# A perceiver layer on one core: products of zeros, another order of the opening, and row sums on GpSimd

## The reference

```python
x = x + xattn(layernorm(x), ctx, top_k=32)      # ctx: 16 x 512 x 512
# xattn: q = n @ Wq.T + bq; k = ctx @ Wk.T + bk; v = ctx @ Wv.T + bv
#   scores = q @ k.T / sqrt(512); all but the 32 largest of a row are dropped
#   softmax, times v, @ Wo.T + bo
x = x + wave(layernorm(x))   # q, k, v, gate; a decaying-cosine kernel per head
#   exp(-softplus(damping) t) * cos(frequency t + phase), heads mixed by softmax(coupling)
x = x + ffn(layernorm(x))    # weights rounded to -1, 0, 1 by their mean magnitude
```

## Time and profile before

| | |
|---|---|
| Median of 3 runs | 445.98 us (445.91 to 446.12) |
| The profiled execution, its own time | 447.19 us |
| Its span in the profile | 445.4 us |
| Busy: TensorE products, weight loads | 433.1 us, 312.7 us |
| Busy: VectorE, ScalarE, GpSimd | 257.6 us, 205.6 us, 111.1 us |
| First product | 4.33 us |
| First context chunk | 50.41 us |

### The profile page before, as it was taken

One profiled execution on the slowest core, in us unless ns is written; L12 is line 12 of the kernel. 1 busy time (PEld: TensorE's weight loads), 2 busy tenths in 40 slices (PEclk: granted clock), 3 DMA queues, 4 the chain that ended last, 5 costly groups with the idle time before them and its releaser, 6 DMA issues.

```text
span 445.4 us, 5681 instructions
## 1 busy us (share of the span) xinstructions
PE 433.1 (97%) x2045; PEld 312.7 (70%) x2045; DVE 257.6 (58%) x519; ACT 205.6 (46%) x305; POOL 111.1 (25%) x163
## 2 busy tenths in 40 slices
PE   5999999999999999899999999999999999999996
PEld 2587644557565655478888888887888888888884
DVE  2988535567766777769987335548753333533334
ACT  1796852645464466538875445435531111111110
POOL 2600440000000002010008603334256633333330
PEclk9999999999999999999999999999999999999999
DMA  6999920675414542225649000000000000200002
GB/s 192 409 379 391 371 80 0 208 266 190 179 46 155 190 156 105 94 96 188 213 166 177 13 22 4 0 0 1 0 1 0 0 1 1 95 1 1 1 0 94
DMA packets 26844, 49.97 MB, mean 112 GB/s; under 512 B 6208, under 2 KB 6208, under 8 KB 25792
## 3 DMA queue, kind: packets, MB, share of 16 engines
q1 hardware_dynamic: 26816, 49.61, 31.7%
HBM read 47.49 MB, written 2.11 MB: 111 GB/s over the span
## 4 chain that ended last, share of the span: by engine, by line
PE 78%; DMA 7%; DVE 6%; ACT 4%; issue 2%; SPq 1%; POOL 1%; DVEq 0%; ACTq 0%
PE bank L1189 10%; PE bank L1191 10%; PE bank L1190 10%; PE bank L1605 7%; PE bank L1603 7%; PE bank L1589 6%; PE bank L1590 6%; PE bank L1384 6%; PE bank L1370 5%; PE bank L1398 5%; PE bank L1297 3%; PE bank L1196 3%; DMA wab<-w1T 2%; DMA wab<-w2T 2%; DVE ln_s L779 1%
## 5 line engine op out<-in xcount | busy, mean ns | idle before, releaser
L754 ACT ACTIVATE g<-bank,b1c 128x512 f32<-128x512 f32 x32 | 22.0, 688 | 92.0 <-PE bank L1605 92.0
L1169 DVE CAST g_hi<-g 128x512 fp32r<-128x512 f32 x32 | 14.0, 436 | 74.7 <-ACT g L754 74.6
L417 POOL TENSOR_TENSOR ln_rs<-ln_ve,neg_half 128x1 f32<-128x1 f32 x24 | 14.9, 620 | 146.2 <-DVE ln_ve L783 145.8
L1603 PE MATMUL bank<-xt_lo,w1s 128*128 128x512 f32 x128 | 50.8, 397 | 0.0
L1605 PE MATMUL bank<-xt_hi,w1s 128*128 128x512 f32 x128 | 50.7, 396 | 0.0
L1589 PE MATMUL bank<-w2s,g_lo 128*128 128x512 f32 x128 | 50.3, 393 | 0.2 <-DVE g_lo L1171 0.2
L1590 PE MATMUL bank<-w2s,g_hi 128*128 128x512 f32 x128 | 50.0, 390 | 0.0
L569 ACT ACTIVATE mt<-bank 128x512 f32<-128x512 f32 x56 | 30.1, 600 | 28.6 <-PE bank L1370 28.6
L464 POOL TENSOR_SCALAR w2s<-w2t 128x512 fp32r<-128x512 int8 x32 | 19.9, 622 | 65.8 <-PE bank L1590 65.8
L1384 PE MATMUL bank<-mt,qT 128*64 128x512 f32 x128 | 31.1, 605 | 0.0
L1589 PEld LDWEIGHTS bank<-w2s,g_lo 128*128 128x128 f32 x128 | 24.0, 188 | 6.1 <-issue 0.6
(11 more groups left out here) (231 smaller groups left out, 1015.3 us busy)
## 6 DMA issues: line engine op xcount, KB each, us to landing
ctxr<-ctx SPq DMA_DIRECT2D x8, 1024.0 KB, 10.9
ctx<-ctx SPq DMA_DIRECT2D x8, 1024.0 KB, 7.7
wab<-w1T SPq DMA_DIRECT2D x4, 1024.0 KB, 11.5
wab<-w2T SPq DMA_DIRECT2D x4, 1024.0 KB, 9.0
wgraw<-wgT SPq DMA_DIRECT2D x4, 1024.0 KB, 6.5
wst<-w1T SPq DMA_DIRECT2D x4, 1024.0 KB, 4.7
wst<-w2T SPq DMA_DIRECT2D x4, 1024.0 KB, 5.2
resid<-x SPq DMA_DIRECT2D x4, 512.0 KB, 6.9
```

The lines of the kernel that those rows point to most:

```text
L1603: pe.matmul(bank[n % 2][:, :], w1s[:, n % 2, d, :], xt_lo[:, d, half(n // FC)], start=(d == 0), stop=False)
```

## The change

- TensorE multiplies a tile of zeros eight times before the first weight step. GpSimd clears that tile (mix_hi, not yet used) first of all.
- The loads: weights of step 1 go ahead of the first x tiles, and each x load goes one step later. The four small wave inputs are issued by ScalarE's queue, after the first weights have landed. Wv goes ahead of magnitude piece 5 instead of 6. The wait for the lag tables goes behind context 7.
- TensorE turns tiles 0 and 1 before step 3, and tiles 2 and 3 between its two halves. Tiles 4 and 5 and the bias products go behind query products 0 and 1, tiles 6 and 7 behind product 2; x_bias goes one product later, norms behind the first four chunks.
- VectorE takes low parts of tiles 0 to 3 and of M before the statistics of tiles 4 to 7; the low parts of tiles 6 and 7 go behind sum_q and the damping chain. [...] norm_part and token sums 4 and 5 go into the first pair.
- GpSimd makes the cosine's arguments after the deviations of all tiles.
- ScalarE's parts follow the same order. Two magnitude passes go ahead of tiles 4 and 5, and passes 6 and 7 go into the first pair.

The diff, without declarations, the count that consts waits for, and function bodies that only change place:

```diff
@@ SyncE
-            def first_loads(o):
+            def first_weights(o):
                 sp.dma_start(wqraw[:, o, :], rows(wq)[:, o, :]).then_inc(wqk_in[o], 16)
                 sp.dma_start(wkraw[:, o, :], rows(wk)[:, o, :]).then_inc(wqk_in[o], 16)
-                if o == 0:
-                    sp.dma_start(cols[:, :, :], small[0]).then_inc(small_in, 16)
-                    for n, a in enumerate((freq, damp, phase)):
-                        sp.dma_start(wpar[:, n, :], a.partition_broadcast(P)).then_inc(par_in, 16)
-                    sp.dma_start(cpl[0:H, :], coup).then_inc(par_in, 16)
+
+            def x_load(o):
+
                 sp.dma_start(resid[:, 2 * o:2 * o + 2, :], x_v[:, 2 * o:2 * o + 2, :]).then_inc(x_in[o], 16)
...
-            for o in range(DC):
-                first_loads(o)
+            first_weights(0)
+            sp.dma_start(cols[:, :, :], small[0]).then_inc(small_in, 16)
+            for o in range(1, DC):
+                first_weights(o)
+                x_load(o - 1)
+            x_load(DC - 1)
...
-                        if k == 2 * DC - 2:
+                        if k == 2 * DC - 3:
                             sp.dma_start(wvraw[:, :, :], rows(wv)).then_inc(wv_in, 16)
...
-                if b == 4:
+                if b == 7:
                     sp.wait_ge(lag_ok, 2)
                     sp.wait_ge(tpos_ok, 5)
@@ GpSimd
+            pool.memset(f(mix_hi[:, :]), 0.0).then_inc(consts, 1)
             link(pool.memset(ident[:, :], 0.0))
...
+            for t in range(NT):
+                rstd(t)
+
             pool.wait_ge(tpos_ok, 4)
             pool.wait_ge(par_in, 64)
...
-            for t in range(NT):
-                rstd(t)
+            def row_sum(to, raw, col, o):
+
+                scale = cols[:, col, o:o + 1]
+                if o == 0:
+                    return pool.tensor_scalar(to[:, :], raw[:, o, :], scale, None, ALU.mult)
+                link(pool.tensor_scalar(row_part[:, :], raw[:, o, :], scale, None, ALU.mult))
+                return pool.tensor_tensor(to[:, :], to[:, :], row_part[:, :], ALU.add)
+
+            pool.wait_ge(wo_in, 16)
+            pool.wait_ge(qbias_ok, 1)
+            for o in range(DC):
+                row_sum(sum_k, woraw, 2, o).then_inc(sums_ok, 1)
+                pool.wait_ge(sums_ok, DC + o + 1)
@@ ScalarE
+            act.wait_ge(wqk_in[0], 32)
+            for n, a in enumerate((freq, damp, phase)):
+                act.dma_start(wpar[:, n, :], a.partition_broadcast(P)).then_inc(par_in, 16)
+            act.dma_start(cpl[0:H, :], coup).then_inc(par_in, 16)
...
-            first_tiles((0, 1, 2, 3, 4, 5))
-            first_xt((0, 1, 2, 3))
-            first_tiles((6, 7))
-            for e in range(DC):
-                m1_hi_part(e)
...
-            first_xt((4, 5))
-            abs_part(0)
-            first_xt((6, 7))
+            first_tiles((0, 1, 2))
+            first_xt((0,))
+            first_tiles((3,))
+            first_xt((1,))
+            m1_hi_part(0)
+            m1_hi_part(1)
+            first_xt((2, 3))
+            m1_hi_part(2)
+            m1_hi_part(3)
+            abs_part(0)
+            abs_part(1)
+            first_tiles((4, 5))
             act.wait_ge(sp_u, 1)
             act.activation(wtmp[:, 1, :], wtmp[:, 0, :], ACT.Exp, scale=-1.0).then_inc(sp_u, 1)
...
+            first_xt((4, 5))
+            first_tiles((6, 7))
             act.wait_ge(qbias_ok, 1)
             q_part(0)
-            abs_part(1)
             q_part(1)
-            abs_part(2)
             act.wait_ge(sumq_ok, DC)
             q_part(2)
+            first_xt((6, 7))
+            abs_part(2)
+            q_part(3)
             abs_part(3)
-            q_part(3)
...
+            q_part(4)
             abs_part(4)
-            q_part(4)
+            q_part(5)
+            q_part(6)
             abs_part(5)
-            q_part(5)
-            abs_part(6)
-            q_part(6)
             q_part(7)
...
                 if i == 0:
+                    abs_part(6)
                     abs_part(7)
+                    act.wait_ge(abs_ok, 2 * DC)
                     wvo_hi_part(0)
@@ VectorE
-            dve.wait_ge(par_in, 64)
...
-            for o in range(DC):
-                sumk_part(o)
-                first_stats((2 * o, 2 * o + 1))
-            first_xt((0, 1, 2, 3))
-            for e in range(DC):
-                m1_lo_part(e)
+            sumk_part(0)
+            first_stats((0, 1))
+            sumk_part(1)
+            first_stats((2, 3))
+            sumk_part(2)
+            first_xt((0, 1))
+            m1_lo_part(0)
+            m1_lo_part(1)
+            first_xt((2, 3))
+            m1_lo_part(2)
+            m1_lo_part(3)
+            first_stats((4, 5))
+            sumk_part(3)
+            first_stats((6, 7))
+            dve.wait_ge(par_in, 64)
...
+            first_xt((4, 5))
             dve.wait_ge(qbias_ps, 1)
             dve.tensor_copy(qbias[:, :], bank[4][:, 0:DC + 1]).then_inc(qbias_ok, 1)
-            first_xt((4, 5))
             for o in range(DC):
                 row_sum(sum_q, wqraw, 1, o).then_inc(sumq_ok, 1)
                 dve.wait_ge(sumq_ok, o + 1)
-            first_xt((6, 7))
...
             link(dve.scalar_tensor_tensor(out=a, in0=q, scalar=2.0, in1=a, op0=ALU.mult, op1=ALU.add))
+            first_xt((6, 7))
...
-            xbias_sum()
             token_part(6)
             token_part(7)
             mix_part()
             token_part(0)
-            xbias_part()
             token_part(1)
...
             token_part(3)
+            xbias_part()
...
                 if i == 0:
+                    norm_part()
+                    token_part(4)
+                    token_part(5)
...
                     wvo_lo_part(0)
@@ TensorE
-            def m1_step(o):
+            def m1_step(o, es=range(DC)):
...
+            pe.wait_ge(consts, 1)
+            for n in range(8):
+                pe.matmul(bank[7][:, 0:P], f(mix_hi[:, :]), f(mix_hi[:, :]), start=True, stop=True)
             for o in range(DC - 1):
                 m1_step(o)
-            pe.wait_ge(consts, 4)
-            for t in range(4):
-                turn_first(t)
-            m1_step(DC - 1)
+            pe.wait_ge(consts, 5)
+            turn_first(0)
+            turn_first(1)
+            m1_step(DC - 1, (0, 1))
+            turn_first(2)
+            turn_first(3)
+            m1_step(DC - 1, (2, 3))
...
+            pe.wait_ge(xt_lo_ok, 4)
+            q_product(0)
+            q_product(1)
             turn_first(4)
             turn_first(5)
-            pe.wait_ge(xt_lo_ok, 4)
-            q_product(0)
+            query_bias()
+            q_product(2)
             turn_first(6)
             turn_first(7)
-            q_product(1)
-            q_product(2)
+            q_product(3)
...
-            for n in range(3, 2 * DC):
+            for n in range(DC, 2 * DC):
                 if n == 5:
                     coupling()
-                if n == 6:
+                if n == 7:
                     x_bias()
-                if n == 7:
-                    norms()
                 q_product(n)
...
                     ln2_turn(i - 3)
+                if i == 0:
+                    norms()
                 score(i, 0)
```

More of the change, by code:

```diff
@@ L145, in perceiver_kernel @@
          (cvt_hi, cvt_lo, gate, bias_2, w1s, w2s, g32, g_hi, g_lo),
-         (wab, turns, sum_k, sum_q, bias_x)) = region(
+         (wab, turns, sum_k, sum_q, bias_x, row_part)) = region(
             [("wvo_hi", [P, DC, D], F32R), ("wvo_lo", [P, DC, D], F32R),
@@ L531, in abs_part @@
                 act.activation(v, v, ACT.Abs, accum_out=wabs[:, k:k + 1]).then_inc(abs_ok, 1)
+            first_tiles((0, 1, 2))
[10 more added lines that the diff above has]
+            first_tiles((4, 5))
+            act.wait_ge(sp_u, 1)
+            act.activation(wtmp[:, 1, :], wtmp[:, 0, :], ACT.Exp, scale=-1.0).then_inc(sp_u, 1)
+            act.wait_ge(cmax_ok, 1)
+            act.activation(cpl[0:H, :], cpl[0:H, :], ACT.Exp, bias=nmax[0:H, :], scale=1.0,
+                           accum_out=rsum[0:H, :]).then_inc(cexp_ok, 1)
             first_xt((4, 5))
-            abs_part(0)
-            first_xt((6, 7))
+            first_tiles((6, 7))
             act.wait_ge(qbias_ok, 1)
             q_part(0)
-            abs_part(1)
             q_part(1)
-            abs_part(2)
             act.wait_ge(sumq_ok, DC)
             q_part(2)
+            first_xt((6, 7))
+            abs_part(2)
+            q_part(3)
             abs_part(3)
-            q_part(3)
             act.wait_ge(dec_ok, 1)
@@ L879, in token_part @@
                                          op0=ALU.mult, op1=ALU.mult, accum_out=ctok[:, t:t + 1]).then_inc(ctok_sum, 1)
-            def xbias_sum():
-                dve.wait_ge(wo_in, 16)
-                dve.wait_ge(qbias_ok, 1)
-                for o in range(DC):
-                    row_sum(sum_k, woraw, 2, o).then_inc(sums_ok, 1)
```

(27 more changed lines are left out.)

32 lines of the change are left out of this document (12 added, 20 removed).

## The result

| | median | runs | profiled execution | its span |
|---|---|---|---|---|
| before | 445.95 us | 445.57 to 446.12 (4) | 447.19 us | 445.4 us |
| changed | 451.92 us | 451.66 to 452.77 (4) | 451.66 us | 449.9 us |

The changed kernel takes 1.0138 times as long as the one before (95% interval 1.0121 to 1.0156), 6.0 us more. The forecast was 452.3 us. The table also shows a difficulty: the profiled execution of before is 1.2 us above its own median, that of the changed kernel is not. The two traces alone therefore show less than the medians do: TensorE's last product starts at 441.12 and at 444.96, 3.8 us apart.

A forecast was written before the change was run, and what follows sets the result against it. TensorE, busy 97%, was taken as the bound. Query product 4 starting +5.6 us later (43.3 for 37.68), less 0.74 and 0.37, plus 1.87 for the clock, gave +6.4 us: median near 452.3 us, range 445.0 to 453.8.

The forecast's parts named there:

- Loads and zeros: Opening: earlier weights and a raised clock start step 1 at 8.3 instead of 10.53, 2.2 us won.
- Rival 4: Opening: zeros don't raise the clock, step 0 takes 5.3 us, later steps 1.9 us later: 454.2 us; chance 0.06.
- TensorE alone: Query product 4: by TensorE's own work it would start at 36.0.
- The wait that I placed ahead of product 0: Query product 0: TensorE ready at 20.5, VectorE's fourth low part ends at 21.0.
- VectorE alone: VectorE's chain before query product 4: tile 7's low part ends at 38.05, product 4 at 38.1, a 2.1 us wait.
- rival 3: Query product 4: tile 7's low part is out before 36.0, needing 2 us off VectorE's chain: 443.2 us; chance 0.07.
- GpSimd: Row sums beside VectorE's sum_q and damping chain: seven instructions hold VectorE up 5.2 us, product 4 at 43.3.
- rival 2: GpSimd's row sums don't disturb VectorE, product 4 starts at 38.1: 445.3 us; chance 0.17.
- Clock: After the long wait ahead of query product 4: TensorE drops to 1.2 GHz, costing 1.87 us.
- Rival 1: Query product 4: the same wait, but the clock holds afterwards: 450.5 us; chance 0.22.
- The later gains: After the opening: 0.74 us won on the last query copies, 0.37 us on context loads 5 to 7.

The follow-up runs named there:

- run 2: Changed kernel with the low parts of tiles 6 and 7 ahead of VectorE's damping chain, row sums still on GpSimd: 454.02 us, ratio to before 1.0171.
- run 1: Changed kernel with the row sums of the output weights back on VectorE: 446.83 us, ratio to before 1.0016.
- run 9: Changed kernel without GpSimd's three row-sum additions, its four scalings kept (output invalid): profiled execution 449.50 us, two executions only, no ratio.
- run 3: Changed kernel with 20 products of the zero tile in the wait ahead of query product 4: 450.09 us, ratio to before 1.0089.
- run 4: Changed kernel without the eight products of zeros, the clearing of their tile kept: 452.71 us, ratio to before 1.0145.
- run 6: Kernel before with the new order of the loads alone, tables on ScalarE's queue: 452.23 us, ratio 1.0140.
- run 7: Kernel before with the zeros and the new order of the loads, nothing else of the change: 451.80 us, ratio 1.0132.
- run 5: Kernel before with the cleared tile and eight products of zeros alone (the run with the zeros): 446.27 us, ratio 1.0010.
- run 12: Kernel before with zeros, new load order, tables on SyncE's queue behind the last x load, and their first readers behind the tiles: 448.0 us, ratio 1.0051.
- run 10: Changed kernel with tiles 6 and 7 ahead of the damping chain, coupling behind product 6, table loads on SyncE's queue: 445.83 us, ratio 0.9997.

## Why the prediction was right

**Sign, size and cause** came out: a wait for tile 7's low part, caused by its new place on VectorE and by GpSimd's sums, then a slow clock. Step by step, with what it measured:

- *Loads and zeros.* Step 1 at 8.3: 8.40, though weights (0.5 us) set it and not step 0. The first x tiles were there at 9.7, not 9.1. The gain against a usual execution is 1.4 us (9.81), not the 2.2 that I took from one profiled execution. Rival 4 fell with step 0 at 3.69 us.
- *TensorE alone.* 36.0 for product 4: 35.97 in run 2. The wait that I placed ahead of product 0 (0.5 us) was 0.6.
- *VectorE alone.* 38.05 for the last low part, 38.1 for product 4: 37.27 in run 1, so this was 0.8 us too much, but not the 2 us that rival 3 needed.
- *GpSimd.* This term was mis-sized: 5.2 us forecast, 3.2 measured (run 1, against which rival 2 falls too). Three additions of 1.09 us each became 1.7 together, since only two met VectorE instructions with both operands in SBUF, at 0.88 and 0.97 us (1.06 and 1.143 against 0.18); the third met the low parts, with an operand in PSUM, and cost nothing. Four scalings of 0.48 became 1.5 together (run 9). The work lasted 11.0 us where I had 6.2: a scaling took 1.58 to 1.77 us, and the int8 row with 0.62 that I used was no guide to it. The Trainium skill's "SBUF — State Buffer" (section "SBUF: two separate sides") has a GpSimd instruction that reads SBUF and a VectorE one with two SBUF inputs hold a shared pair of ports by an exclusive lock, for the whole instruction; by it the prediction had 6.2 us. The trace agrees with it that a low part with one operand from PSUM is free, and that an addition holds the VectorE instruction beside it until it ends (34.93 for 34.90, 37.95 for 37.92). It does not agree for the scalings: those of 1.6 us cost 0.38 us each, and beside them VectorE ran most of its 128x16 products at 0.176 us.
- *Clock.* 1.87 forecast, 1.5 in the trace (4.55 us from product 4 to the coupling, 3.01 in run 1; 4.22 against 2.68 in run 3). It was taken from the opening, and held in mid-kernel. Rival 1 of the prediction (the clock holds) falls with it.
- *The later gains.* 0.74 and 0.37: the two waits are gone, a new one of 0.3 for ScalarE's copy of a turned context (mt) came; from the coupling to the last product the changed kernel is 0.8 us ahead of the run with the zeros.
- *The tail*, 0.6 us, was not in the sum at all, and why it is longer stays open. I charged the four table loads 1.9 us of ScalarE's idle time and nothing at the end.

Against the run with the zeros: product 4 started there at 36.87, 2.90 us ahead of the coupling. (The same row of the kernel before is 37.58; the prediction had 37.68.) The later start is 40.75 - 36.87 = 3.9; product 4 itself takes 1.65 more, 1.5 of it the clock; less 0.8; tail 0.6: 5.4 us, which is 451.66 - 446.26.

So the mechanism was right, and that the median came out within 0.4 us is partly luck. Too much was forecast for GpSimd (2.0 us), for VectorE's own chain (0.8) and for the clock (0.3). Against that, the tail (0.6) was not seen, the later gains were 0.3 less, the trace of before that the sum starts from was 0.7 us late, and the two medians lie 0.6 us further apart than the two profiled executions compared above. The range has a slip too: the 6.2 us named as its upper end give 453.3 by the sum, not 453.8; both hold the result. For the profiled execution of the changed kernel I had said 453.5, and it took 451.66: the 1.2 us by which the one of before lay above its median was no property of profiling.

## What to carry to other kernels

Read a long dependent chain by all its deadlines: moving two tiles ahead of it brought the first demand 4.8 us forward and made a wait of 5.3 at the second, and only moving the consumer too gave the time back. Price the work that another engine does beside such a chain by what each of its instructions meets, not by its length: here an addition cost the chain 0.9 us or nothing, and a longer scaling 0.4. Put it beside instructions with a PSUM operand, or where the chain has slack. Look at the granted clock behind a group of short waits as well as behind a long one. And before an execution is used as the base of a sum, see whether it is a usual one; one late landing of weights shifted this base by 0.7 to 0.9 us, as much as the changed kernel wins behind the coupling (0.8).

## What the runs showed of the hardware

- Behind a wait of 4.2 us the granted clock was still 1.00 and fell to 0.50 only 0.6 us after the next product's start, at 41.4 (changed kernel), or 1.2 us after it, at 43.3 (run 4). Behind 2.5 us it fell 0.4 us after the start (run 9). In the wait of 5.3 us it fell during the wait, at 43.8, 0.9 us ahead of the next product (run 2). Behind a wait of 1.0 us it did not fall (run 1), but it did at 21.7 behind four waits of 0.7 to 0.8 us, some 0.65 us of work apart (run 6).
- The stretch at 0.50 lasted 3.4 us in the changed kernel and in runs 4, 6, 7 and 9, and 6.8 in run 2.
- A GpSimd addition of two 128x512 tiles held a VectorE instruction with both operands in SBUF until it ended, which cost 0.88 and 0.97 us; a scaling cost such an instruction 0.2 to 0.4 us; two low parts with one operand in PSUM took their usual 1.29 us beside an addition.
- GpSimd's scaling of 128x512 floats by a column took 1.58 to 1.77 us, longer than its addition of two such tiles, 1.26 to 1.30.
- A load of 1 KB took 7.5 us from issue to landing where it went out amid the weights and tokens, on ScalarE's queue (run 6), and 3.4 where SyncE issued it ahead of most of them (run 5). On SyncE's own queue behind the last x load it took 9.1 (run 12), so no second queue is needed to make it late.
- Using ScalarE's queue for four loads in the first 7 us went with a tail that is 0.6 us longer and one instruction packet in it, in nine kernels of nine, and in none of the five without; run 10 has it back at 4.28 by moving these loads alone. What in the queue's use does it was not tried.
